# Window attention and a dynamic convolution on one core: the transposed attention output goes to another PSUM bank, the residual x is added by an accumulating transfer, and the last convolution runs one strip later in the part without attention

## The reference, cut to what matters

```python
def _L0_conv_ref(x0, ...):
    x = layernorm2d(x0, ln_w, ln_b)
    qk, vs = conv1x1(x, qk_w, qk_b), conv1x1(x, vs_w, vs_b)
    q, k = (qk[:, :ADIM], qk[:, ADIM:])
    local = depthwise3x3(vs, depth_w) + depth_b[None, :, None, None]
    v1, v2 = (vs[:, :ADIM], vs[:, ADIM:])
    # q, k, v1 rolled by -4 in both directions, cut into 8x8 windows, 4 heads
    atn = jax.nn.softmax(jnp.einsum('nhqc,nhkc->nhqk', qw, kw) * SCALE, axis=-1)
    y = jnp.concatenate([rolled_back(einsum('nhqk,nhkc->nhqc', atn, vw)), v2], axis=1)
    s = (y + local).mean(axis=(2, 3), keepdims=True)
    ca = sigmoid(conv1x1(leaky_relu(conv1x1(s, fu1_w), 0.2), fu2_w))
    y = y * ca + local * (1.0 - ca)
    return conv1x1(y, proj_w, proj_b) + x0

def _L1_conv_ref(x, ...):
    t = relu(batchnorm(x.mean(axis=(2, 3)) @ w1.T))
    wt = (t @ w2.T + b2) * MASK     # taps (-1,-1) (-1,0) (-1,1) (0,-1) are left
    return depthwise3x3(x, wt) + bias
```

## Time and profile before

| | |
|---|---|
| median of 3 runs | 1499.13 us |
| the profiled execution | 1503.79 us |
| its span, first to last instruction | 1502.2 us |
| busy in the span: PE, DVE, ACT, POOL | 88%, 84%, 58%, 15% |
| attention alone | 39 to 299.5 us |
| main stage, 48 strips | 299.5 to 1303.5 us |
| tail | 1303.5 to 1502 us |

### The profile page before, as it was taken

The page is one execution under the profiler, slowest core; times in us unless marked ns, Lnnn a source line. Parts: engine busy times, 40 slices in busy tenths (PEclk is TensorE's granted clock), DMA queues, the critical chain, the costliest instruction groups (busy, mean ns, idle before and its releaser), DMA issues.

```text
span 1502.2 us, 38208 instructions
## 1 busy us (share of the span) xinstructions
PE 1323.6 (88%) x12403; PEld 782.0 (52%) x12403; DVE 1263.8 (84%) x2222; ACT 875.8 (58%) x2279; POOL 230.8 (15%) x741
## 2 busy tenths in 40 slices
PE   5989898889899999989899999988989998888986
PEld 3666666555555555555555555555555555433332
DVE  3565656479999999999999999999989998999998
ACT  2566666666666666776566666765666666622221
POOL 2111111111122211221111211220112011000000
PEclk9999999999999999999999999999999999999999
DMA  2121212345665566645655566646655664678884
GB/s 62 51 82 55 81 55 81 99 98 148 167 148 144 138 152 165 156 114 154 166 147 139 138 159 156 156 114 159 155 125 141 161 155 112 164 181 195 211 199 126
DMA packets 81357, 203.07 MB, mean 135 GB/s; under 512 B 15248, under 2 KB 19112, under 8 KB 81320
## 3 DMA queue, kind: packets, MB, share of 16 engines
q1 hardware_dynamic: 81320, 202.60, 53.9%
HBM read 136.57 MB, written 64.91 MB: 134 GB/s over the span
## 4 chain that ended last, share of the span: by engine, by line
PE 36%; ACT 20%; DVE 16%; issue 13%; DMA 13%; ACTq 1%; DVEq 0%; SPq 0%; POOL 0%; POOLq 0%
DMA qd<-nmx 12%; PE banks_s L521 9%; ACT pt L811 5%; PE banks_t L529 5%; PE banks_t L483 5%; ACT km L767 4%; DVE mx L1009 4%; ACT ybuf L799 4%; PE banks_g L612 4%; PE banks_g L496 4%; DVE mixed L1181 3%; PE banks_g L614 3%; DVE oo L1192 3%; ACT vw L780 2%; DVE zs L1204 2%
## 5 line engine op out<-in xcount | busy, mean ns | idle before, releaser
L1181 DVE SCALAR_TENSOR_TENSOR mixed<-vin,c_pack,mixed 96x1024 f32<-96x1024 f32 x352 | 450.0, 1278 | 6.6
L1192 DVE SCALAR_TENSOR_TENSOR oo<-zs,l_w,oo 96x1024 f32<-96x1024 f32 x192 | 245.1, 1276 | 8.3 <-ACT oo L847 4.1
L811 ACT ACTIVATE pt<-banks_t 128x512 f32<-128x512 f32 x256 | 138.6, 593 | 129.0 <-PE banks_t L529 127.5
L1009 DVE TENSOR_REDUCE mx<-banks_s 128x8 f32<-128x512 f32 x260 | 167.6, 687 | 48.1 <-PE banks_s L521 47.3
L529 PE MATMUL banks_t<-qd,km 64*128 64x128 f32 x2048 | 152.8, 290 | 30.1 <-DMA qd<-nmx 30.0
L521 PE MATMUL banks_s<-km,qd 64*128 64x128 f32 x2080 | 152.9, 286 | 18.9 <-issue 15.2
L980 DVE BATCH_NORM_STATS2 bn<-banks_a 128x6 f32<-128x96 f32 x528 | 99.0, 249 | 80.5 <-PE banks_a L471 80.1
L521 PEld LDWEIGHTS banks_s<-km,qd 64*128 64x128 f32 x2080 | 129.7, 189 | 70.7 <-DVE mx L1009 40.4
L612 PE MATMUL banks_g<-vin,proj_t 128*96 128x512 f32 (+1 forms) x288 | 150.2, 622 | 11.4 <-DMA ycat<-y_img 5.7
L529 PEld LDWEIGHTS banks_t<-qd,km 64*128 64x128 f32 x2048 | 127.9, 192 | 49.9 <-issue 26.1
L434 POOL COPY vrow<-vw 96x16 f32<-96x16 f32 (+2 forms) x520 | 153.4, 349 | 0.0
(11 more groups left out here) (148 smaller groups left out, 1842.5 us busy)
## 6 DMA issues: line engine op xcount, KB each, us to landing
vin<-v_img SPq DMA_DIRECT2D x64, 495.0 KB, 5.9
v_img<-vrow SPq DMA_DIRECT2D x130, 198.0 KB, 2.8
xc<-in_x SPq DMA_DIRECT2D x134, 192.0 KB, 2.6
x<-in_x SPq DMA_DIRECT2D x64, 384.0 KB, 7.2
out<-oo SPq DMA_DIRECT2D x64, 384.0 KB, 3.0
y_img<-ybuf SPq DMA_DIRECT2D x128, 99.0 KB, 2.0
ycat<-v_img SPq DMA_DIRECT2D x64, 198.0 KB, 4.9
ycat<-y_img SPq DMA_DIRECT2D x64, 198.0 KB, 7.0
```

The costliest lines, as they stand in the source:

```text
L811: fn(pt[:, 2 * r + n, :], banks_t[:, n, :], ACT.Exp).then_inc(pt_done, 1)
L1009: v.tensor_reduce(mx[:, n, :, 4 * r:4 * r + 4].rearrange("q h e -> q e h"), banks_s[:, n, :].rearrange("q (e h k) -> q e h k", h=2, k=K), ...
L1181: v.scalar_tensor_tensor(out=mb[:C, par, :, 0:W], in0=vin[:C, par, 1 + dh:1 + dh + WS, 1 + dw:1 + dw + W], scalar=depth_w[:, DVE_TAPS[m]:D ...
L1192: v.scalar_tensor_tensor(out=oo[:, par, :, :], in0=zs[:, at:at + WS, 1 + dw:1 + dw + W], scalar=l1_w[:, n:n + 1], in1=oo[:, par, :, :], op ...
```

## The change

1. DVE's `finish` is gone. ACT's new `z_out` reads the projection from PSUM, adds the bias and writes `zs` at the head of its strip. GpSimd then issues a transfer that adds x from memory to `zs` (`add_x`, `accum_op=ALU.add`), after one small instruction on a tile `rest` that keeps its own order. The separate load of x and its tile are gone.
2. `zs` is two separate buffers with a halo row each, so that ACT copies the halo every strip. The side columns are gone: ACT's first tap is now (-1, 0), and the three taps on DVE that shift by a column cover 127 of 128 columns.
3. In the tail, the last convolution of a strip (`tap0`, `l1`, the store) comes one strip later than before.
4. `y_transposed` writes the second bank of `banks_t`, behind the second half of the values; `yq` has two buffers, and ACT's `y_out` stands after the maxima. On SP `store_y` moves to the strip's end.
5. In the main stage the transfer of the maxima is issued by ACT, right behind `nmx`. ACT's `rsqrt` stands ahead of `keys`, the sums of an image after `y_out`; PE's second x transposition is ahead of the second half of the transposed scores; DVE takes both maxima of a half in one instruction, and the statistics' second half before the third mix.

```diff
+            def add_x(u, par):                                   # POOL
...
+                pool.wait_ge(add_turn, FREE + u)
+                pool.wait_ge(zs_done, u + 1)
+                nc.gpsimd.tensor_tensor(rest[:], rest[:], rest[:], ALU.add).then_inc(add_turn, 1)
+                pool.dma_start(zs[:, par, 1:1 + WS, :], x[b, :, bass.ds(j * WS, WS), :],
+                               accum_op=ALU.add).then_inc(x_added[par], 16)
...
+            def z_out(u, par, late=False, after=None):           # ACT
+                act.wait_ge(z_done, u + 1)
...
+                fn(zs[:, par, 1:1 + WS, :].rearrange("c r x -> c (r x)"), of[:C, :, :].rearrange("c a n -> c (a n)"),
+                   ACT.Identity, bias=z_bias[:]).then_inc(zs_done, 1)
+
+            def tap0(u, um, par, after=None):
+                act.wait_ge(x_added[par], 16 * (um + 1))
+                act.wait_ge(halo_done, u + 1)
...
             def maxima_out(s, k):
...
                 fn(nmx[:], ps_mx, ACT.Copy, scale=-1.0).then_inc(nmx_done, 1)
+                act.wait_ge(nmx_done, s + 1)
+                act.dma_start(qd[62:66, k, :, :, :].rearrange("j p w q -> j (p w q)"), nmx[:]).then_inc(mx_moved, 16)
...
             def strip(...):                                      # ACT
+                if prev:
+                    z_out(u - 1, k, late, after)
...
+                if prev and not late:
+                    tap0(u - 1, h - NS // 2 - 1, k, after)
...
+                if late and after is None:
+                    tap0(u - 2, h - NS // 2 - 2 + k, 1 - k, before)
+                    halo(u - 1, k)
...
+                if attend:
+                    maxima_out(t + 1, 1 - k)
+                    y_out(t - 1, 1 - k, h - 1 + k)
                 if gate is not None:
                     image_sums(gate)
-                if attend:
-                    maxima_out(t + 1)
...
-                for n in range(2):                               # DVE, maxima
-                    v.tensor_reduce(mx[:, n, :, 4 * r:4 * r + 4].rearrange("q h e -> q e h"),
+                v.tensor_reduce(mx[:, :, :, 4 * r:4 * r + 4].rearrange("q n h e -> q n e h"),
...
-            def finish(u, um, par, late=False):                  # DVE
...
-            def last(h, k):
-                for m in range(NT - 1):
+            def last(h, k, old=True):
+                for m in range(NT):
                     mix(u, par, m, True)
-                finish(u - 1, h - NS // 2 - 1, k, late=True)
-                mix(u, par, NT - 1, True)
-                for n in range(1, NL + 1):
-                    l1(u - 1, k, n)
+                if old:
+                    for n in range(1, NL + 1):
+                        l1(u - 2, par, n)
...
                 if ahead:                                        # SP, strip
+                    load_strip(t - LAG + 1, k, prev, gate, t - 1 if attend else None, k)
+                if late and older:
+                    store_out(t - LAG - 3, k)
```

More of the change, by code:

```diff
@@ L344, in _, with strip @@
             move_max(0, 0)
-            def strip(h, k, attend=True, y=True, ahead=False, prev=False, older=False, gate=None):
+            def strip(h, k, attend=True, y=True, ahead=False, prev=False, older=False, gate=None, alone=False, late=False):
                 t = 2 * h + k
-                if older:
+                if older and not late:
                     store_out(t - LAG - 2, 1 - k)
@@ L630, in alone @@
                 pe.wait_ge(yq_done, FREE + 2 * t)
+                if not (isinstance(t, int) and t < 2):
+                    pe.wait_ge(y1_done, YO * (t - 1))
                 scores_transposed(k, 0)
@@ L693, in strip @@
                 if attend:
[L694 removed]
+                    pe.wait_ge(mx_done, 2 * (t + 1) + 1)
                     scores(1 - k, 1)
[L696 removed]
+                    values(t, k, 1)
+                    y_transposed(t - 1, 1 - k)
                     pe.wait_ge(yq_done, FREE + 2 * t + 1)
@@ L904, in projections, with strip @@
                 fn(proj_m[C:128, :], projT[of[2], :], ACT.Copy, scale=free[2]).then_inc(proj_done, 1)
-            def strip(h, k, attend=True, y=True, ahead=False, prev=False, gate=None, gated=None):
+            def strip(h, k, attend=True, y=True, ahead=False, prev=False, gate=None, gated=None, late=False, after=None, before=None):
                 t = 2 * h + k
                 u = t - LAG
+                if prev:
+                    z_out(u - 1, k, late, after)
                 if attend:
@@ L912, in strip @@
                     vs_out(t + 1, 1)
-                if y:
+                if y and not attend:
                     y_out(t - 1, 1 - k, h - 1 + k)
@@ L949, in _ @@
             strip(NS // 2, 1, ahead=True, gated=0)
-            with act.Fori(NS // 2 + 1, NS) as h:
+            strip(NS // 2 + 1, 0, ahead=True, prev=True, after=0)
+            strip(NS // 2 + 1, 1, ahead=True, prev=True)
+            with act.Fori(NS // 2 + 2, NS) as h:
                 for k in range(2):
@@ L956, in _ @@
                 strip(h0, 1, ahead=True, prev=True, gated=b - 1)
-                with act.Fori(1, NS // 2) as hh:
+                strip(h0 + 1, 0, ahead=True, prev=True, after=b - 1)
+                strip(h0 + 1, 1, ahead=True, prev=True)
+                with act.Fori(2, NS // 2) as hh:
                     for k in range(2):
@@ L962, in _ @@
             strip(h0, 1, attend=False, y=False, ahead=True, prev=True, gated=B - 1)
-            with act.Fori(h0 + 1, h0 + NS // 2) as h:
+            strip(h0 + 1, 0, attend=False, y=False, ahead=True, prev=True, late=True, after=B - 1)
+            strip(h0 + 1, 1, attend=False, y=False, ahead=True, prev=True, late=True, before=B - 1)
+            with act.Fori(h0 + 2, h0 + NS // 2) as h:
                 for k in range(2):
-                    strip(h, k, attend=False, y=False, ahead=True, prev=True)
-            strip(h0 + NS // 2, 0, attend=False, y=False, prev=True)
+                    strip(h, k, attend=False, y=False, ahead=True, prev=True, late=True)
+            strip(h0 + NS // 2, 0, attend=False, y=False, prev=True, late=True)
+            z_out(B * NS - 1, 1, late=True)
+            tap0(B * NS - 2, B * NS // 2 - 1, 0)
+            halo(B * NS - 1, 1)
             tap0(B * NS - 1, B * NS // 2 - 1, 1)
@@ L1292, in strip @@
                     l1(u - 1, k, 3)
+                if gate is not None and attend:
+                    local_mean(gate)
+                    squeeze_in(gate)
                 if gated is not None:
@@ L1315, in _ @@
             strip(h0, 1, attend=False, cur=True, prev=True, gated=B - 1, tail=True)
-            with dve.Fori(h0 + 1, h0 + NS // 2) as h:
+            last(h0 + 1, 0, old=False)
+            last(h0 + 1, 1)
+            with dve.Fori(h0 + 2, h0 + NS // 2) as h:
                 for k in range(2):
@@ L1319, in _ @@
             last(h0 + NS // 2, 0)
-            finish(B * NS - 1, B * NS // 2 - 1, 1, late=True)
-            for n in range(1, NL + 1):
-                l1(B * NS - 1, 1, n)
+            for u in (B * NS - 2, B * NS - 1):
+                for n in range(1, NL + 1):
+                    l1(u, u % 2, n)
 def kernel(**inputs):
```

208 lines of the change are left out of this document (107 added, 101 removed).

## The result

The changed kernel takes **1488.78 us** (median of 5 runs, 1487.66 to 1499.47) against 1499.29 us for the kernel before beside it. The ratio is 0.9934, 95% interval 0.9905 to 0.9963. On a second chip the same pair gave 0.991 (0.9881 to 0.994). So it is faster by 0.7 to 0.9%, some 10 to 14 us, where 24 were forecast. The time lies inside the range of 1440 to 1507; most of the forecast's gain did not come.

A forecast was written before the change was run, and what follows sets the result against it. Hand-to-hand latency in a loop over PE and ACT bounds the main stage, DVE the tail. Terms -16 + 6 - 3 - 11.4 = -24.4 us from the profiled 1503.8 give 1479.4, as a median 1475 us; range 1440 to 1507.

The forecast's parts named there:

- the plain strips: Main stage: loop over ACT and PE summed to 20.6 us against 20.99, over 42 plain strips 16 us less.
- the issue: Main stage: ACT issuing the maxima's transfer behind `nmx` was taken at 0.68 us, the median of that issue on SP.
- DVE is no bound, by itself this gives nothing: Main stage: one 1.28 us pass leaves DVE, its need falls to about 17.8 us a strip, gaining nothing by itself.
- Gate strips, +2 us x 3 = 6 us: At three image borders the image's sums now stand behind `y_out` in the loop: +6 us, between 0 and 12.
- Tail, -11.4: Tail: 14 strips from 10.39 to 9.4 us, 13.9 us less, and +2.5 at the end, together -11.4 us.
- Its steady part: Tail strips: transfers fill 8.6 to 10.2 us, taken as 9.4 against 10.39 us a strip, 13.9 us less over 14.
- the prediction's signs: Tail: seven DVE passes with idle time between them, and PE waiting for y, at 9.2 to 9.6 us a strip.
- "+2.5" for the end: End of the tail: `z_out` 1.2, x's transfer 4.5 and the same taps, partly hidden behind the strip before: +2.5 us.
- the reckoning of x's landing: Main stage, before `tap0`: GpSimd's instruction, issue and a 7.1 us load make 8.5 of 9.5 us allowed; costed at nothing.
- The first, a hidden issue: Main stage: issue on ACT hidden or `z_out` cheap, strip 19.9 us, 29 us more go, 1446 us; chance 0.22.
- The second, x too late: Main stage, ACT's `tap0` and DVE's first tap: x 1.5 us late in 48 strips, 72 us, 1547 us; chance 0.12.
- The third: Work moves, sum stays: ACT's loop 20.9 to 21.0 us, tail transfers 10.2 us and more, 1505 us; chance 0.20.

The follow-up runs named there:

- three cuts: Changed kernel with SyncE issuing the maxima's transfer, with late rows copied ahead of the maxima, or with the `zs` copy cut to 8 columns: 0.9765, 0.9701, 0.9691.
- experiments 5 and 6: Changed kernel with copies and sums ahead of the maxima in border strips alone, 1475.59 us; changed kernel with x's transfer plain, not accumulating, 1486.95 us.
- the eighth experiment: Kernel before the change, with DVE's sum of projection, bias and x into `zs` cut to 8 columns: 1477.41 us, ratio 0.9839.

## Why the prediction was wrong

**Right, the plain strips.** The new loop over ACT and PE was summed to 20.6 us, and measured 20.7 (869.3/42). Its bound, vs waiting for `zs`, is what three cuts confirm. Two terms were off and partly cancelled: the issue 0.99 and not 0.68, `z_out` 1.11 and not 1.23. In the first two images the gain is 0.35 us a strip (589.1 to 579.4 us) where 0.39 was worked out. The 24.7 us gained are more than 16 because before's third image is some 10 us longer than its other two; two of its strips, of 23.8 and 25.5 us, run in part at the lower clock, each behind a wait of PE for the maxima's transfer:

```profile
1263.23 2.08 PE L529 MATMUL banks_t<-qd,km 64*128 64x128 f32 x16 [2.07 <-DMA qd<-nmx]
1265.24 3.73 PE L496 MATMUL banks_g<-xn,c_pack 96*96 96x512 f32 x4
```

The other wait is 1.79 us (1112.32). The prediction had no term for that, so this part of the gain is luck. In after, where ACT issues the transfer, the longest such wait is 1.24 us and no plain strip loses the clock, in either profile. Whether that is the change's doing is not shown: the kernels of experiments 5 and 6, which issue it in the same way, have one such strip each in the third image (22.9 and 24.2 us), the first of them behind waits of only 0.89 and 0.76 us. The step "DVE is no bound, by itself this gives nothing" held in the main stage: the eighth experiment.

**Wrong, the term "Gate strips, +2 us x 3 = 6 us"**: measured +15.8 for the three pairs. The 2 us of sums were placed rightly. What failed is pricing them as if only their length counted. At the second and third border they came on top of PE's wait for `zs`, 3.08 and 3.37 us in a row without work. Behind that PE ran at 1.2 GHz for 17.1 us at the second, where the pair grew by 7.7 us, and for 3.4 us at the third, where it grew by 3.6; at the first it ran so for 17.1 us against 6.8 in before, and the pair grew by 4.6. So with hardly any lower clock a border costs nearly twice the 2 us, and the clock comes on top; how wait and clock share the rest is not separated. Moving sums and copies gives back 19.4 us of the profile, and the ratio of 0.9934 (0.991 on the second chip) became 0.9818: more than the 9.8 us that this term was off, since the copies go out of the border's loop as well.

**Wrong, the term "Tail, -11.4"**: measured +1.8. Its steady part was right, 9.4 us forecast and 9.38 measured over the last 12 strips, from 10.39, with DVE and PE busy 92 and 94% and PE waiting for y, as the prediction's signs had it (1364 to 1477 us):

```profile
PE banks_t L641 <- DMA ycat<-y_img: 4.1, 6, 1.3
PE banks_g L641 <- DMA ycat<-y_img: 2.6, 4, 1.2
```

Its frame was not. (a) "+2.5" for the end was +5.4: the last transfer of x, with 4.52 us of waiting, is followed by all of a strip's taps, and little hides behind the strip before. The transfer itself was sized well, 4.9 us where 4.5 was taken. And before's last strip, from one `zs` to the last, took only 6.42 us, after's 9.48, another 3.1 us that the forecast did not have. (b) The border without attention was costed at nothing, though there `tap0` follows `z_out` with no attention between: ACT waits 3.40 and 6.93 us for x, +4.3 up to the 16th `zs`. TensorE is at its lower clock there for longer too, some 20 us between 1298 and 1326 us, where before has 6.8 us at its border; no run separates the two. (c) The three strips right behind take 31.4 us, no less than before's, and one of them 13.3 us instead of 9.4: PE waits 2.58 us for y in it. With x's bytes taken out that strip takes 9.9 us. That x's transfer, the burst of loads and the store meet there is argued and not shown; x's 5.77 MB in 140 us are 22.1% of the transfer engines' time, beside 67.1% for the rest, where the earlier trace rows had 83.0% in all. The step that failed is the reckoning of x's landing in the steady state alone, at 7.1 us beside others; it is 5.0 in the main stage and 8.2 in the tail.

**The rivals.** The first, a hidden issue, did not occur: the issue costs more than was taken. Its number, 19.9 us a strip, is what comes when it is taken off ACT. The second, x too late, is false in the main stage, where no wait of ACT for x is listed between 360 and 1290 us; it is true where no attention covers it. It was put at the wrong place. The third had ACT's loop at 20.9 to 21.0 us and the tail's strips at 10.2 and more; neither came. Its 1505 us lies 16 us above the result, the forecast 14 below.

**On what hid the small instruction of GpSimd.** In after L463, GpSimd's instruction ahead of x's transfer, takes 1049 ns on the mean (20 times, 494 to 900 us), while L438 on a tile of the same size takes 191, where the earlier trace rows had 686 and 189. This agrees with the rule of the Trainium skill named before the result ("SBUF — State Buffer", "Who interferes with whom"), if L463 falls beside DVE's two-input passes and L438 between them. The Trainium skill's figure for a transfer from GpSimd ("DMA: Bandwidth & Descriptors", "Anatomy of one DMA — SWDGE (gpsimd) path") gave an estimate of 2.9 us for x. Plain transfers of that size take 3.9 here, accumulating ones 5.0, and one of 3 KB in the tail 5.9; with nothing beside it one of 3 KB takes 2.2 and the accumulating one of x 4.9. By the measurement, x's landing beside other transfers is not to be worked out from its bytes.

## What to carry to other kernels

When work goes onto an engine whose total is low, ask where in its list it stands: 1.8 us of copies behind a hand-off lengthen the loop, and put ahead of it, into idle time, they took 0.6 us off the strip before the next limit was met. At borders and at the end of a stage, walk the loop again without the work that covered the new latency; a transfer that is free in the steady state is exposed there. And where a term lengthens a wait of TensorE, price the clock behind it too, not only the wait, as a range: here 3.08 us of wait were followed by 17.1 us at the lower clock, 3.37 us by 3.4.

## What was not expected of the hardware

- A transfer issued by ACT, whose queue entry shows 0.65 us, takes 0.99 us out of ACT's list when it must wait for ACT's own instruction just before.
- A wait of TensorE of 3.08 us, in place of the 0.94 of a plain strip, was followed by 17.1 us at 1.2 GHz, one of 3.37 us by 3.4 us; with 0.58 in the same place the clock stayed at 2.4 GHz. In the fifth kernel waits of 0.89 and 0.76 us in one plain strip were followed by 3.4 us at 1.2 GHz.
- An accumulating transfer of 384 KB lands 1.1 us later than a plain one (5.0 and 3.9), and one of 3 KB takes 5.9 in a busy stretch and 2.2 with nothing beside it.
